# Attention in a four-layer kernel: the split maxima go into the query slot in three SBUF transfers instead of one round trip through DRAM, and the next block's loads are issued behind them

## The chip, the cores and the metric

The kernel is one program on one core of one Trainium2 chip. The metric is the device time of one execution in microseconds (us). Before the change, three runs took 3569.54, 3575.7 and 3576.92 us; the median is 3575.7 us.

## The reference

Four layers run over 32 blocks of 256 tokens with 128 features: a state-space layer and an expert layer, linear attention and experts, softmax attention with low-rank experts, and a scan followed by a small transformer layer with experts. The change touches only the two softmax attentions, `h2` (causal, layer 2) and `h3` (not causal, layer 3). What they compute per block is this (`h3` in the reference's own words; `h2` is the same with a causal mask and low-rank projections):

```python
q, k, v = (heads(q), heads(k), heads(v))        # 16 heads of 8
scores = jnp.einsum('bhqd,bhkd->bhqk', q, k) / jnp.sqrt(jnp.asarray(hd, x.dtype))
attn = jax.nn.softmax(scores, axis=-1)
o = jnp.einsum('bhqk,bhkd->bhqd', attn, v)
return o @ wo.T + bo
```

## The kernel before, in words

`attend(tag, ...)` runs once for `h2` and once for `h3`. The loop is over blocks `b` of 256 tokens (32 of them), software-pipelined over three blocks at once, and written out for each engine by hand: step `b` computes, for each of 16 head positions `h`, the weights of block `b` (`scores`, `weights`, `weigh`), the row maxima of block `b + 2` (`max_scores` on TensorE, `maximum` on VectorE), and the end of block `b - 1` (`turn_sums`, `norm`, `turn_out`, `project_out`, `added`). All engines work through their own list in order; semaphores are all that ties them. A `Signal` named `s["x"]` counts; `at("x", b, k)` is its value after `k` of block `b`'s counts.

Queries and keys are held as three bf16 parts of each number, 48 rows (`KR = 48`) in all, so that a bf16 matmul over 128 partitions gives scores of nearly f32 precision. There are four slots, `sq[u]` and `sk[u]`, each 128 partitions x 16 heads x 256 tokens bf16; block `b` uses slot `b % 4`. Rows 48 to 50 of a query slot (`KR:KM`) are special. Rows 48 to 50 of the key slots hold ones. While a block's maxima are being computed its query rows 48 to 50 are zero. Later they hold the negated maximum of each query, split into three bf16 parts, so that the same matmul gives score minus maximum, ready for `Exp`.

The maxima take this path. VectorE reduces them (`h_nm`); GpSimd splits them into three parts (`split_max`, `h_mpart`); at head position 5 of step `b` TensorE turns the parts of block `b + 1` (`turn_max`, line 2387) and ScalarE copies them to `mT`, 48 partitions (part by head) x 256 tokens (line 2460, signal `mc`). SyncE's queue then stores `mT` to the DRAM tensor `m_parts` (line 2166, signal `mout`), waits for that, and loads `m_parts` into rows 48 to 50 of block `b + 1`'s query slot (line 2168, signal `min`). TensorE's first `scores` of step `b + 1` wait for `min`.

SyncE's queue also loads block `b + 3`: queries (line 2482, 48 x 16 pieces of 512 bytes), keys (line 2483, the same), zeros for rows 48 to 50 (line 2484, copied from a zero part of `sk[0]`) and values with a column of ones (line 2153, 256 pieces of 576 bytes). It does that in step `b` as soon as `weigh` of block `b - 1` is over (signal `pv`), at head position 2. These four transfers count on one signal, `loaded` (64 = 4 x 16). The first `max_scores` of step `b + 1`, at head position 0 right behind the first `scores`, works on block `b + 3` and waits for all 64 (`unit_free`). The steps before block 1 load nothing, since four blocks lie in the slots when the loop starts, and the last three have nothing left to load.

In SyncE's step the loads stand ahead of the two `m_parts` transfers.

Of the kernel before, what the change touches and what calls it, by code (L numbers as in the profile page):

```python
# [33 lines left out]
NH, HD = 16, 8  # L34
# [138 lines left out]
def build(nc, x_in, pack_in, maskb_in, w0_in, w1_in, w3_in, out, ktab, ychan, q_stack, k_stack, ones_rows, v_ones,  # L173
          m_parts, xs1, xs3, ys):
    ctx = ExitStack()
    with ctx:
# [5 lines left out]
        def sig(name, per):  # L182
            return Signal(pool, name, per)

        def sb(name, shape, dt=F32, stack=ctx):
            return stack.enter_context(nc.sbuf_tensor(name, shape, dt))
# [101 lines left out]
        for t, nf, choices in (("e1", F1 // P, 2), ("e3", F3 // P, 1)):  # L288
# [22 lines left out]

        attns = {t: dict(
            {k: sig(f"{t}_{k}", n) for k, n in (
                ("s1", units), ("mx", units), ("mf", 1), ("ms", 3), ("ml", 1), ("mt", 1), ("mc", 1), ("mout", 16), ("min", 16),
                ("vp", 2), ("s2", NH), ("ex", NH), ("pv", 4), ("ev", 2), ("tu", 2), ("rec", 2), ("on", 2), ("ot", 1),
                ("otc", 1), ("out", 1), ("x", 1))},
            loaded=[SlotSignal(pool, f"{t}_loaded{u}", 64, u + 4, 4) for u in range(4)]) for t, units in (("h2", 6), ("h3", 8))}
# [621 lines left out]
        with ExitStack() as st_d:  # L939
# [3 lines left out]
            with ExitStack() as st:  # L943
                mx = sb("d_max", [P, NT], stack=st)
# [950 lines left out]
        with ExitStack() as st1:  # L1895
            h_all = sb("h_all1", [P, NT * P], stack=st1)
            s1, s2 = (sb(f"m1_sel{j}", [P, NT, E1], stack=st1) for j in range(2))
# [31 lines left out]
        KR = 6 * HD  # L1929
        KM = KR + 3  # L1930
# [166 lines left out]
        def attend(tag, causal, dst, w, buffers, load):  # L2097

            s = attns[tag]
# [4 lines left out]
            def at(name, b, k):  # L2104

                return s[name].now(b, k)

            def head(h):

                g, j = h // HG, h % HG  # L2110
                return 8 * (g // 2) + 2 * j + g % 2

            with ExitStack() as st:
                sq, sk, mskb = (buffers[n] for n in ("sq", "sk", "mskb"))
# [5 lines left out]
                mT = sb(f"{tag}_mT", [3 * NH, SEQ], BF16, stack=st)  # L2120
# [13 lines left out]
                def run(eng, step):  # L2134
                    for b in range(-2, 1):
                        step(b, b % SLOTS, b // SLOTS, first=True, turn=b >= -1, body=b >= 0, tail=False)
                    with eng.Fori(0, (NB - 4) // SLOTS) as i:
                        for v in range(1, SLOTS + 1):
                            step(i * SLOTS + v, v % SLOTS, i + v // SLOTS, first=True, turn=True, body=True, tail=True)
                    for b in range(NB - 3, NB + 1):  # L2140
                        step(b, b % SLOTS, b // SLOTS, first=b + 2 < NB, turn=b + 1 < NB, body=b < NB, tail=True)

                def ahead(u, r, n):

                    return (u + n) % SLOTS, r + (u + n) // SLOTS

                with pool.loop_block(NB) as block:
                    k_set = n_chain[0] + 4

                    @block.sync  # L2150
                    def _(sp):
                        def load_values(b, u, up):
                            sp.dma_start(vb[u][:, :, :, :].rearrange("p t h e -> p t (h e)"),
                                         v_ones[ds(b * TPB, TPB)].rearrange("t p w -> p t w")).then_inc(up, 16)

                        def step(b, u, r, first, turn, body, tail):
                            if first and tail and not (isinstance(b, int) and b + 3 >= NB):
                                sp.wait_ge(*at("pv", b, 0))
                                slot = ahead(u, r, 3)[0]
                                load(sp, b + 3, slot, s["loaded"][slot].sem)  # L2160
                                load_values(b + 3, slot, s["loaded"][slot].sem)
                            if turn:

                                sp.wait_ge(*at("mc", b + 1, 1))
                                sp.wait_ge(*at("min", b + 1, 0))
                                sp.dma_start(m_parts.rearrange("a h t -> (a h) t"), mT[:, :]).then_inc(s["mout"].sem, 16)
                                sp.wait_ge(*at("mout", b + 1, 16))
                                sp.dma_start(sq[ahead(u, r, 1)[0]][KR:KM, :, :], m_parts).then_inc(s["min"].sem, 16)

                        for b in range(SLOTS):  # L2170
                            load_values(b, b, first_v[tag])
                        run(sp, step)
# [103 lines left out]
                    def _(pe):  # L2276
# [66 lines left out]
                        def scores(b, u, h):  # L2343

                            if h == 0:
                                pe.wait_ge(*at("min", b, 16))
                            pe.wait_ge(*at("ex", b, h - 1))
                            o, hd = ps_2[:, h % 2, :], head(h)
                            if causal:
                                pe.matmul(o[:, 0:SEQ], sk[u][:, hd, 0:P], sq[u][:, hd, :], start=True, stop=False, skip_group_check=True)  # L2350
                                pe.matmul(o[:, SEQ:SW], sk[u][:, hd, P:2 * P], sq[u][:, hd, P:], start=False, stop=False,
                                          skip_group_check=True)
                                ins = pe.matmul(o.rearrange("p (t q) -> p t q", q=SEQ)[:, :, 0:P], mskb[:, 0:P],  # L2353
                                                mskb[:, 2 * P:3 * P].unsqueeze(1).to_broadcast([P, 2, P]),
                                                start=False, stop=True, skip_group_check=True)
                            else:
                                for t in range(TPB):
                                    ins = pe.matmul(o[:, t * SEQ:(t + 1) * SEQ], sk[u][:, hd, t * P:(t + 1) * P], sq[u][:, hd, :],  # L2358
                                                    start=True, stop=True)
                            ins.then_inc(s["s2"].sem, 1)  # L2360
# [76 lines left out]
                    @block.scalar  # L2437
                    def _(act):
                        def weights(b, h):
                            g, j = h // HG, h % HG  # L2440
                            act.wait_ge(*at("s2", b, h + 1))
                            if j == 0:
                                act.wait_ge(*at("pv", b, g - 1))
                            act.activation(pt[g % 2][:, j, :], ps_2[:, h % 2, 0:SW], ACT.Exp, scale=scale).then_inc(s["ex"].sem, 1)  # L2444

                        def keep_sums(b, k):
                            act.wait_ge(*at("pv", b, 2 * k + 2))
                            act.wait_ge(*at("tu", b, k - 1))
                            act.activation(sums[k][:, :], ps_o, ACT.Copy).then_inc(s["ev"].sem, 1)

                        def step(b, u, r, first, turn, body, tail):
                            for h in range(NH):
                                if body:
                                    weights(b, h)
                                if h == 3 and tail:
                                    keep_sums(b - 1, 1)
                                if h == 5 and turn:
                                    act.wait_ge(*at("mt", b + 1, 1))
                                    act.wait_ge(*at("mout", b + 1, 0))
                                    act.activation(mT[:, :], ps_m[0:3 * NH, :], ACT.Copy).then_inc(s["mc"].sem, 1)  # L2460
                                if h == 11 and body:
                                    keep_sums(b, 0)
                                if h == 12 and tail:
                                    act.wait_ge(*at("ot", b - 1, 1))
                                    act.wait_ge(*at("out", b - 1, 0))
                                    act.activation(oT[:, :], ps_m, ACT.Copy).then_inc(s["otc"].sem, 1)

                        run(act, step)


        stats(x_res)
        heads_in = dict(
            sq=[sb(f"h_sq{u}", [P, NH, SEQ], BF16) for u in range(SLOTS)],
# [47 lines left out]
        with ExitStack() as st2:  # L2521
# [4 lines left out]
            with ExitStack() as st:  # L2526
                s1, s2, ex = (sb(f"m2_sel{j}", [P, NT, E2], stack=st) for j in range(3))
# [445 lines left out]
```

## Time and profile before

| | |
|---|---|
| median of 3 runs | 3575.7 us |
| the profiled execution | 3574.73 us, its span 3572.9 us |
| TensorE (PE) busy | 2609.7 us (73%) |
| VectorE (DVE) busy | 2245.5 us (63%) |
| ScalarE (ACT) busy | 1580.3 us (44%) |
| GpSimd (POOL) busy | 634.1 us (18%) |
| one load of a block | 384 KB queries, 384 KB keys, 24 KB zeros, 144 KB values |
| one store or load of `m_parts` | 24 KB |
| attention `h2`, its loop | about 1880 to 2345 us |
| attention `h3`, its loop | about 2713 to 3185 us |

The profiled execution is within 1 us of the median, so its durations can be used as they are. Times in the rows are from the span's start. A timeline row gives start, duration, engine, line, instruction, output and input, and in brackets the idle time ahead of it with what ended it. SPq is the queue of SyncE: its rows show when a transfer is issued, not when it lands. PE is the matmul, PEld the weight load. Matmuls overlap, so a PE that is busy all the time is not a PE at its peak. In a row of a table by stretches the columns are the stretch, its length, the busy time of PE, PEld, DVE, ACT and POOL with the number of instructions, the TensorE clock that was granted (1.00 is full), the busy share of the DMA engines, and GB/s.

### The profile page before, as it was taken

How to read it: one execution, taken by the hardware profiler on the slowest of the kernel's cores; microseconds unless marked ns; L12 is line 12 of the kernel's file. 1: busy time of each engine (PE TensorE's matmuls, PEld its weight loads, DVE VectorE, ACT ScalarE, POOL GpSimd, SP SyncE). 2: the span in 40 equal slices, each digit the busy share in tenths (PEclk: the TensorE clock that was granted, in tenths of full speed). 3: DMA queues.
4: the chain of work that ended last, by engine and by line, in shares of the span. 5: the costliest groups of instructions: out<-in, count | busy, mean ns of one | idle time of the engine just before them, and what ended most of it. 6: DMA issues, size and time to landing. Idle time of an engine off the chain costs nothing. (4 is left out here: it accounts for less than half of the span.)

```text
span 3572.9 us, 72294 instructions
## 1 busy us (share of the span) xinstructions
PE 2609.7 (73%) x20194; PEld 1892.7 (53%) x20194; DVE 2245.5 (63%) x4945; ACT 1580.3 (44%) x3615; POOL 634.1 (18%) x873
## 2 busy tenths in 40 slices
PE   3546749999987576998339999966565999973280
PEld 1333444459877433998226777756333555552270
DVE  5924966248777422776846666645885777765267
ACT  2503613334364233775235666632253667751253
POOL 0000100000000265554301111100120111102553
PEclk7878959999998687999679999968797999985585
DMA  3096100100091011222494565400097555510123
GB/s 94 7 258 176 53 0 18 35 18 0 0 156 54 20 46 43 70 69 89 152 276 62 71 73 71 57 1 1 0 293 109 69 68 75 71 43 19 53 77 100
DMA packets 335935, 263.34 MB, mean 74 GB/s; under 512 B 23132, under 2 KB 317452, under 8 KB 335308
## 3 DMA queue, kind: packets, MB, share of 16 engines
q1 hardware_dynamic: 314200, 227.03, 31.5%
q0 software_dynamic: 12928, 26.70, 2.2%
q10 hardware_dynamic: 8704, 8.39, 0.8%
q8 instruction: 46, 0.75, 0.1%
q14 instruction: 57, 0.47, 0.0%
HBM read 145.60 MB, written 114.86 MB: 73 GB/s over the span
## 5 line engine op out<-in xcount | busy, mean ns | idle before, releaser
L2444 ACT ACTIVATE h_pt<-h_ps 128x384 f32<-128x384 f32 (+1 forms) x1024 | 543.6, 545 | 306.2 <-PE h_ps L2353 151.8
L2197 DVE TENSOR_REDUCE h_nm<-h_ps 128x4 f32<-128x1024 f32 (+1 forms) x448 | 539.7, 1220 | 163.4 <-PE h_ps L2324 64.0
L1606 POOL DMA_INDIRECT sorted_rows<-e_row,e_pos x192 | 185.1, 964 | 443.4 <-DVE e_row L1585 239.6
L2372 PE MATMUL h_ps_o<-h_pt,h_vp 128*32 128x256 f32 (+1 forms) x4096 | 246.8, 358 | 1.3 <-ACT h_pt L2444 1.3
L1796 POOL DMA_INDIRECT results<-e_y,e_ykey x208 | 211.0, 1015 | 193.6 <-DVE e_y L1785 176.7
L1843 ACT ACTIVATE e_hid<-e_ps_h,e_wt 128x128 f32<-128x128 f32 x688 | 204.3, 369 | 27.7 <-PE e_ps_h L1817 19.0
L2358 PE MATMUL h_ps<-h_sq,h_sk 128*128 128x256 bf16 x1024 | 193.6, 275 | 23.9 <-DMA h_sq<-m_parts 13.6
L1817 PE MATMUL e_ps_h<-e_hT,e_wt 128*128 128x128 f32 x1376 | 201.9, 288 | 6.3 <-issue 2.6
L1825 PE MATMUL e_ps_o<-e_wt,e_hid 128*128 128x128 f32 x1376 | 198.0, 283 | 11.2 <-ACT e_hid L1843 10.4
L1753 DVE TENSOR_SCALAR e_wt<-w 128x1156 f32 (+1 forms) x208 | 140.0, 673 | 98.5 <-DVE e_y L1785 69.8
L1817 PEld LDWEIGHTS e_ps_h<-e_hT,e_wt 128*128 128x128 f32 x1376 | 179.7, 201 | 14.2 <-issue 10.4
L1825 PEld LDWEIGHTS e_ps_o<-e_wt,e_hid 128*128 128x128 f32 x1376 | 178.2, 199 | 15.9 <-ACT e_hid L1843 13.5
L2295 PE MATMUL h_ps<-h_sk,h_sq 128*128 128x256 bf16 x1024 | 157.1, 277 | 39.7 <-DVE h_identb L2179 34.5
L2243 POOL TENSOR_TENSOR h_mpart<-h_nm,h_zero 128x32 bf16<-128x32 f32 x64 | 15.3, 240 | 892.5 <-DVE h_nm L2197 892.5
L2372 PEld LDWEIGHTS h_ps_o<-h_pt,h_vp 128*32 128x32 f32 x4096 | 106.8, 109 | 92.5 <-issue 36.7
L1810 PE MATMUL e_ps_t<-pack,e_xt 128*128 128x128 f32 x208 | 59.2, 286 | 124.9 <-DMA e_xt<-sorted_rows 124.3
L2350 PE MATMUL h_ps<-h_sq,h_sk 128*128 128x256 bf16 x512 | 140.6, 275 | 6.6 <-ACT h_pt L2444 2.8
L2353 PE MATMUL h_ps<-h_mskb 128*128 128x256 bf16 x512 | 139.6, 273 | 0.0
L1140 DVE TENSOR_TENSOR x_hid<-x_gelu,x_ps_u 128x512 f32<-128x512 f32 x64 | 43.4, 688 | 141.8 <-ACT x_gelu L1125 141.8
L2307 PE MATMUL h_ps<-h_sk,h_sq 128*128 128x256 bf16 x512 | 98.2, 274 | 45.7 <-DVE h_identb L2179 44.3
L2358 PEld LDWEIGHTS h_ps<-h_sq,h_sk 128*128 128x128 bf16 x1024 | 81.5, 98 | 93.1 <-ACT h_pt L2444 80.6
L2295 PEld LDWEIGHTS h_ps<-h_sk,h_sq 128*128 128x128 bf16 x1024 | 98.4, 99 | 58.7 <-DVE h_identb L2179 34.7
(435 smaller groups left out, 6170.8 us busy)
## 6 DMA issues: line engine op xcount, KB each, us to landing
h_sq<-q_stack SPq DMA_DIRECT2D x64, 384.0 KB
h_sk<-k_stack SPq DMA_DIRECT2D x64, 384.0 KB
sorted_rows<-pad SPq DMA_DIRECT2D x26, 520.0 KB, 11.7
e_xt<-sorted_rows SPq DMA_DIRECT2D x104, 130.0 KB, 2.2
e_got<-results SPq DMA_DIRECT2D x24, 512.0 KB, 5.9
q_stack<-p_parts SPq DMA_DIRECT2D x32, 384.0 KB, 3.1
k_stack<-p_parts SPq DMA_DIRECT2D x32, 384.0 KB, 3.8
v_ones<-p_v SPq DMA_DIRECT2D x32, 288.0 KB, 2.7
```

The source lines that it names most:

```text
L1606: gp.indirect_dma_start(xs[:, :], bass.IndirectOffsetOnAxis(ap=pos[:, n % choices, tile:tile + 1], axis=0), row[n % ROWS][:, :], None).the ...
L1753: dve.tensor_scalar(wt[j % 4][:, :], w[:, :, :].rearrange("p e w -> p (e w)")[:, ds(at, wc)], 1.0, None, ALU.mult).then_inc(e_w.sem, 1)
L1796: gp.indirect_dma_start(ys[:, :], bass.IndirectOffsetOnAxis(ap=key[m // 4][:, m % 4:m % 4 + 1], axis=0), y[m][:, :], None).then_inc(return ...
L1817: pe.matmul(ps_h[:, k, 0:P], wt[j % 4][:, f * P:(f + 1) * P], hT[j % 4][:, :], start=True, stop=True).then_inc(e_h.sem, 1)
L1825: ins = pe.matmul(o, hid_t[m][:, f, :], wt[m][:, f_dim + f * D:f_dim + (f + 1) * D], start=(f == 0), stop=(f == nf - 1))
L1843: act.activation(hid_t[j % 4][:, f, :], ps_h[:, (j * nf + f) % 4, 0:P], func, bias=wt[j % 4][:, o_b1 + f:o_b1 + f + 1]).then_inc(e_a.sem, 1)
L2197: dve.tensor_reduce(to, got, AX, ALU.max, negate=True).then_inc(s["mx"].sem, 1)
L2295: ins = pe.matmul(ps_1[:, h % 4, q * SEQ:(q + 1) * SEQ], sq[u][:, h, q * P:(q + 1) * P], sk[u][:, h, :], start=True, stop=True)
L2350: pe.matmul(o[:, 0:SEQ], sk[u][:, hd, 0:P], sq[u][:, hd, :], start=True, stop=False, skip_group_check=True)
L2358: ins = pe.matmul(o[:, t * SEQ:(t + 1) * SEQ], sk[u][:, hd, t * P:(t + 1) * P], sq[u][:, hd, :], start=True, stop=True)
L2372: ins = pe.matmul(ps_o[32 * j:32 * (j + 1), q0:], vp[u % 2][:, t, head(HG * g + j), :], pt[g % 2][:, j, t * SEQ:(t + 1) * SEQ - q0], start ...
L2444: act.activation(pt[g % 2][:, j, :], ps_2[:, h % 2, 0:SW], ACT.Exp, scale=scale).then_inc(s["ex"].sem, 1)
```

## The change

Lines 2157 to 2161 of the new kernel take the place of lines 2162 to 2168 of the old one. The detour through `m_parts` and its signal `mout` are gone. `mT` goes straight into the query slot in three transfers, one for each of the three rows: 16 partitions of 512 bytes become one partition of 8 KB. All three count on `min`, which goes to 48. They are issued ahead of the loads of block `b + 3`, so that these loads, the zeroing of rows 48 to 50 and the values come behind them in SyncE's list, and behind its wait for `mc`.

```diff
-                ("s1", units), ("mx", units), ("mf", 1), ("ms", 3), ("ml", 1), ("mt", 1), ("mc", 1), ("mout", 16), ("min", 16),
+                ("s1", units), ("mx", units), ("mf", 1), ("ms", 3), ("ml", 1), ("mt", 1), ("mc", 1), ("min", 48),
@@ SyncE
                         def step(b, u, r, first, turn, body, tail):
+                            if turn:
+
+                                sp.wait_ge(*at("mc", b + 1, 1))
+                                for a in range(3):
+                                    sp.dma_start(sq[ahead(u, r, 1)[0]][KR + a:KR + a + 1, :, :], mT[a * NH:(a + 1) * NH, :]
+                                                 ).then_inc(s["min"].sem, 16)
                             if first and tail and not (isinstance(b, int) and b + 3 >= NB):
                                 sp.wait_ge(*at("pv", b, 0))
                                 slot = ahead(u, r, 3)[0]
                                 load(sp, b + 3, slot, s["loaded"][slot].sem)
                                 load_values(b + 3, slot, s["loaded"][slot].sem)
-                            if turn:
-
-                                sp.wait_ge(*at("mc", b + 1, 1))
-                                sp.wait_ge(*at("min", b + 1, 0))
-                                sp.dma_start(m_parts.rearrange("a h t -> (a h) t"), mT[:, :]).then_inc(s["mout"].sem, 16)
-                                sp.wait_ge(*at("mout", b + 1, 16))
-                                sp.dma_start(sq[ahead(u, r, 1)[0]][KR:KM, :, :], m_parts).then_inc(s["min"].sem, 16)
@@ TensorE, scores
-                                pe.wait_ge(*at("min", b, 16))
+                                pe.wait_ge(*at("min", b, 48))
@@ ScalarE, the copy to mT
-                                    act.wait_ge(*at("mout", b + 1, 0))
+                                    act.wait_ge(*at("min", b + 1, 0))
```

No instruction of TensorE, VectorE, ScalarE or GpSimd moves. On SyncE's queue one step of the loop of `attend` reads so before (ISA and REGISTER_ALU rows are waits and address arithmetic; signal5 is `pv`, signal3 is `mc`, signal2 is `min`, signal4 is `mout`):

```order
L2482 ISA [waits signal5]
L2482 DMA h_sq<-q_stack 48x16x256
L2483 DMA h_sk<-k_stack 48x16x256
L2484 DMA h_sq<-h_sk 3x4096
L2153 ISA
L2153 DMA h_vb<-v_ones 128x2x144
L2164 REGISTER_ALU
L2165 ISA [waits signal2]
L2166 DMA m_parts<-h_mT 48x256 [waits signal3]
L2167 REGISTER_ALU
L2168 DMA h_sq<-m_parts 3x4096 [waits signal4]
```

The same step of SyncE's queue after the change, where the lines of the loads have moved up by one, signal2 is `mc` and signal4 is `pv`:

```order
L2159 REGISTER_ALU
L2161 DMA h_sq<-h_mT 1x16x256 [waits signal2]
L2161 DMA h_sq<-h_mT 1x16x256 x2
L2164 ISA
L2481 ISA [waits signal4]
L2481 DMA h_sq<-q_stack 48x16x256
L2482 DMA h_sk<-k_stack 48x16x256
L2483 DMA h_sq<-h_sk 3x4096
L2153 ISA
L2153 DMA h_vb<-v_ones 128x2x144
```

The four loads have moved from ahead of the wait for `mc` to behind it and behind three transfers; the wait for `mout`, which stood between the last two rows, is gone.

## Rows read from the trace of the kernel before

**Rows 1.** The page, its head.

```profile
span 3572.9 us, 72294 instructions
```

**Rows 2.** Windows of `h2`'s middle, `h3`'s middle and `h3`'s end.

```profile
1922.00:2316.00 394.00, 389.92 (x4668) 288.43 (x4666) 250.29 (x362) 247.24 (x557) 50.21 (x168) 1.00 0.56 70
...
2750.00:3130.00 380.00, 361.72 (x3736) 225.49 (x3734) 298.54 (x401) 264.87 (x533) 47.83 (x160) 1.00 0.56 71
3130.00:3185.00 55.00, 48.13 (x496) 26.91 (x488) 26.36 (x47) 37.59 (x77) 4.40 (x14) 1.00 0.16 21
```

**Rows 3.** Tile `h_sq`, what its matmuls waited for: us, times.

```profile
  DMA h_sq<-m_parts: 17.9, 32
```

**Rows 4.** Timeline of SyncE's queue, one step of `h2` and the next.

```profile
2009.68 0.34 SPq L2482 DMA_DIRECT2D h_sq<-q_stack  x1
...
2011.57 0.41 SPq L2153 DMA_DIRECT2D h_vb<-v_ones  x1
2012.45 0.34 SPq L2166 DMA_DIRECT2D m_parts<-h_mT  x1
2018.86 0.26 SPq L2168 DMA_DIRECT2D h_sq<-m_parts  x1
...
2026.52 0.34 SPq L2166 DMA_DIRECT2D m_parts<-h_mT  x1
```

**Rows 5.** Timeline of ScalarE and TensorE in the same steps of `h2`.

```profile
2011.96 0.36 ACT L2460 ACTIVATE h_mT<-h_ps_m 48x256 bf16<-48x256 f32 x1
...
2021.38 0.38 PE L2307 MATMUL h_ps<-h_sk,h_sq 128*128 128x256 bf16 x2
```

**Rows 6.** Timeline of SyncE's queue and TensorE, one step of `h3`.

```profile
2941.24 0.25 SPq L2168 DMA_DIRECT2D h_sq<-m_parts  x1
...
2943.61 0.39 PE L2358 MATMUL h_ps<-h_sq,h_sk 128*128 128x256 bf16 x2 [0.42 <-DMA h_sq<-m_parts]
...
2943.84 0.60 PE L2295 MATMUL h_ps<-h_sk,h_sq 128*128 128x256 bf16 x4
...
2946.38 0.34 SPq L2482 DMA_DIRECT2D h_sq<-q_stack  x1
...
2949.09 0.34 SPq L2166 DMA_DIRECT2D m_parts<-h_mT  x1
```

**Rows 7.** The same queue and TensorE where the maxima came latest in `h3`.

```profile
2760.04 0.34 SPq L2482 DMA_DIRECT2D h_sq<-q_stack  x1
...
2770.64 0.25 SPq L2168 DMA_DIRECT2D h_sq<-m_parts  x1
...
2772.89 0.39 PE L2358 MATMUL h_ps<-h_sq,h_sk 128*128 128x256 bf16 x2 [1.91 <-DMA h_sq<-m_parts]
...
2775.66 0.34 SPq L2482 DMA_DIRECT2D h_sq<-q_stack  x1
```

**Rows 8.** Tile `h_vb`, issue to landing; then windows of a half microsecond in `h2`.

```profile
DMA to landing us min/median/max: 5.9/7.2/8.3
...
2017.50:2018.00 0.50, 0.50 (x8) 0.41 (x7) 0.00 (x0) 0.33 (x2) 0.00 (x0) 1.00 0.76 107
2018.00:2018.50 0.50, 0.50 (x6) 0.43 (x5) 0.27 (x1) 0.50 (x2) 0.00 (x0) 1.00 0.09 22
```

**Rows 9.** Issues by line (ns min/median/max), and four in a row before `h2`.

```profile
L2484 SPq DMA_DIRECT2D h_sq<-h_sk x64: 708/723/3305, 1853.9 to 3131.5; - x64
L2166 SPq DMA_DIRECT2D m_parts<-h_mT x64: 302/339/345, 1890.7 to 3160.5; - x64
...
1851.07 1.68 SPq L2081 DMA_DIRECT2D h_sk<-ones_rows  x4
```

**Rows 10.** Loads of the loops: count; the last of `h2`, the first of `h3`.

```profile
L2482 SPq MOVE h_sq<-q_stack x56: 29/29/37, 1909.2 to 3130.5; - x56
...
2292.60 0.34 SPq L2482 DMA_DIRECT2D h_sq<-q_stack  x1
...
2745.83 0.35 SPq L2482 DMA_DIRECT2D h_sq<-q_stack  x1
```

## The prediction, made before the result was known

> **What bounds the kernel now.** I first read the head of the page for the span, 3572.9 us [rows 1]; the execution took 3574.7 us, so 1.8 us lie around the span, and it stands 1 us under the median of the runs, 3575.7 us. The change touches only the loops of the two attentions, so next come the windows over their middles [rows 2]: TensorE is busy 389.9 of 394 us in `h2` and 361.7 of 380 us in `h3`, at a granted clock of 1.00. VectorE and ScalarE have a quarter or more free. TensorE sets the pace of both loops, and anything that makes it stop is paid. Third, the view of the tile `h_sq` says what TensorE and its weight loads stopped for: the transfer of the maxima out of `m_parts`, 17.9 us in 32 waits over both attentions [rows 3]. That is the wait which the change aims at, and all there is of it.
>
> Fourth, SyncE's queue beside TensorE, step by step. I call q the moment at which the first load of a step is issued. In a step of `h2` [rows 4] q is 2009.68. The values are issued at q + 1.89, and the store of the maxima at q + 2.77. That store follows ScalarE's copy, which ends at 2011.96 + 0.36 = 2012.32 [rows 5], by 0.13 us, so it is the maxima that are late there and not the queue. The store has landed at 2018.86, q + 9.18, when the second transfer is issued. TensorE starts the maxima of the newly loaded block at 2021.38, q + 11.70 [rows 5].
>
> The loads themselves are the thing to place. The values take 7.2 us in the median from issue to landing [rows 8], and 1.89 + 7.2 makes q + 9.1. The DMA engines bear it out: their share falls from 0.76 to 0.09 at 2018.0, q + 8.3, and the last pieces have still to be acknowledged [rows 8]. So a load needs 9.1 us from its first issue, with the DMA engines full of it, and before the change it is ready 11.7 - 9.1 = 2.6 us ahead of its reader. That margin is what the change draws on.
>
> **The change part by part.**
>
> *The three transfers in place of the round trip.* Before, the maxima arrive so: store, landing 6.4 us later because it stands behind a whole load (2012.45 to 2018.86, rows 4), second transfer, and TensorE goes on 2.25 to 2.4 us after that one's issue (2770.64 to 2772.89 in rows 7, 2941.24 to 2943.61 in rows 6). After, they are issued on an empty queue at the same 0.13 us behind the copy, and even at three times 2.4 us one after another they would be there in 7.2 us, where the next step's first maxima, right behind its first scores, are 2021.38 - 2012.45 = 8.9 us away. The 17.9 us of waiting go. Part of that is the weight load's count beside the matmul's for one and the same stop, so I credit 16 us at most, and that only if nothing else is late at the same place. ScalarE's new wait, for `min` instead of `mout`, is for transfers of the step before and is long met: 0. The wait for 48 instead of 16 costs nothing in itself.
>
> *The loads behind them.* Their issue was q; it becomes q + 2.77 in `h2` (2949.09 - 2946.38 = 2.71 in `h3`, rows 6) plus X, the time in which SyncE issues three transfers. X is not in the trace. An issue of the nearest shapes takes 0.34 us (the store of `mT`) or 0.72 us (the other SBUF to SBUF transfer), and four in a row from DRAM take 1.68 us, 0.42 each [rows 9]. With the gaps and the address arithmetic, X lies between 1.1 us (three at 0.34 and little else) and 2.5 us (three at 0.72 and 0.3). I take 1.5: three at 0.42, the row with transfers back to back, and some 0.25 us between. Then the load lands at q + 2.77 + 1.5 + 9.1 = q + 13.4, and TensorE asks for it at q + 11.7. Behind that wait on TensorE stands all the rest of its step: the scores of head 1, for which ScalarE waits, and the maxima, for which VectorE waits. The cover of 2.6 us is gone and 1.7 us are missing.
>
> *Does it repeat?* Yes, since a circle closes: copy of the maxima at head 5, three issues, the load, the wait at head 0 of the next step, TensorE's work from head 0 to head 5, the next copy. Its length is X + 9.1 + R. R is read from the start of the maxima at head 0 to the next store of `mT`: 2026.52 - 2021.38 = 5.14 us in `h2` [rows 4, 5] and 2949.09 - 2943.84 = 5.25 us in `h3` [rows 6]. So the step is 1.5 + 9.1 + 5.14 = 15.74 us in `h2` and 15.85 us in `h3`. Before, 27 steps of `h2` take from 1909.2 to 2292.60, 14.2 us each, and 27 of `h3` from 2745.83 to 3130.5, 14.25 us each [rows 10].
>
> *Does TensorE catch up?* The trace has a step in which the maxima came late by themselves, and TensorE stood for 1.91 us [rows 7]. That load was issued at 2760.04 and the next at 2775.66, 15.62 us apart: 1.4 us over the mean, and from TensorE's restart at 2772.89 to the next q it took 2.77 us, as in a common step, from 2943.61 to 2946.38 [rows 6]. A stop at this place is handed on in full. The new stop lies a little later, behind the first scores, so that ScalarE works off head 0 meanwhile. That may give back what TensorE spends waiting for it between head 0 and 5: I take 0.05 us in `h2`, where TensorE has almost no gap, and 0.2 us in `h3`, with 0 and 0.5 as the ends.
>
> *The sum.* `h2` loses 15.69 - 14.20 = 1.49 us in a step and `h3` 15.65 - 14.25 = 1.40 us. There are 56 loads inside the loops, 28 in each [rows 10], so 28 x 1.49 + 28 x 1.40 = 42 + 39 = 81 us. The gain on the maxima lies inside that, because the period before contains those waits and the period after doesn't. At the start of the loops, outside these 56 steps, 1 us of waiting for the maxima is saved (of the 16, all but those in the middles). The granted clock stays: in `h3`'s end TensorE is busy 48.1 of 55 us and has 1.00 all the same [rows 2], and 1.5 us in 15.7 is no larger hole than that. Sum: 3574.7 + 81 - 1 = 3654.7 us; against the median of the runs, 1 us more. I say 3655.
>
> The ends: X = 1.1, a load of 8.3 us (the fall of the DMA share) and 0.5 us caught up give a step of 1.1 + 8.3 + 5.2 - 0.5 = 14.1, which is no loss. X = 2.5, a load of 9.3 and nothing caught up give 17.0, or 56 x 2.8 = 157 us more, 3732 us.
>
> **The rivals.**
>
> *The load lands in time, and the gain on the maxima is what is left.* The load would have to be faster without the maxima's store behind it. For: the store and the second transfer leave the DMA queue, and a part of 9.1 us is acknowledgement. Against: the shift of 2.77 us alone is already above the margin of 2.6 us, before any of the three issues, and the departing store is 24 KB beside 936 KB. The time would be 3574.7 - 16 = 3558.7, say 3559 us. It decides where a load takes less than 11.7 - 2.8 - 1.5 = 7.4 us.
>
> *A load at the fabric's rate.* If the DMA engines moved this load at their full rate, it would land some 4 to 5 us after its issue, at q + 9, ahead of its reader, and the time would be the 3559 us of the case above. The rows speak against it: 9.1 us, with the engines busy to the end [rows 8]. [...]
>
> *The issues of the three transfers are dear.* One partition takes all 16 pieces, and if SyncE needs 0.72 us for each, as for the other SBUF to SBUF transfer [rows 9], with its gaps X is 2.5 us and the step 16.7 us, the sum 3574.7 + 28 x 2.45 + 28 x 2.4 = 3711 us. For it: the kind of the transfer. Against it: the 0.72 us stand right behind two large issues, and the store of the same `mT` takes 0.34.
>
> *Nearly nothing.* The load closes up to about 8.3 us and the issues are short, so that the stop costs what the maxima cost before: a step of 14.1 to 14.3 us, 3570 to 3580 us.
>
> **How the numbers follow.** The stop on the loads has 0.88: 0.70 around 3655 (3615 to 3690), 0.18 with dear issues or a longer load, up to 3732. The load in time has 0.06 together with the full rate, of which that has 0.01. Nearly nothing has 0.06. A difference under 0.2%, 7 us, is what a measurement of this kernel can't tell from none. So faster 0.06, the same 0.05, slower 0.89. The range of 8 in 10 is 3603 to 3708: it leaves out the cases without a stop and the far part of the dear ones.
>
> **What would show it.** In the profile after, TensorE's first maxima of a step (line 2306 or 2294) carry an idle time of 1 to 2 us ended by a load of `h_sq`, `h_sk` or `h_vb`, 56 times; the waits for the maxima's transfer are gone; the loads are issued 15.6 to 15.8 us apart and about 1.5 us behind the first of the three transfers; TensorE is at about 90% in both middles at an unchanged clock; nothing outside the two loops moves. I would be wrong if the steps are 14 us apart, if the load lands in clearly less than 9 us from its issue, or if TensorE makes up the stop before head 5.

## The result, and the profile after

The changed kernel takes 3736.6 us in the median of 4 runs (3724.52 to 3739.57), the kernel before 3572.8 us in runs beside it. The ratio is 1.0452, with a 95% interval of 1.0424 to 1.0479. The forecast was 3655 us and a range up to 3708: the direction was right, the loss is twice the forecast one, 164 us instead of 80.

The head of the page of the changed kernel, which answers to [rows 1]:

```profile
span 3733.4 us, 72223 instructions
```

Its windows over the middles of the two loops, with the columns of [rows 2]:

```profile
1922.00:2316.00 394.00, 343.83 (x3876) 248.74 (x3874) 210.73 (x303) 205.09 (x462) 42.22 (x142) 0.95 0.47 58
2850.00:3230.00 380.00, 324.57 (x3078) 199.91 (x3079) 246.21 (x327) 218.06 (x439) 39.18 (x131) 0.91 0.45 57
```

TensorE went from 389.9 to 343.8 busy us in the same 394 us of `h2`. And the granted clock has changed: it is 0.95 and 0.91, where both middles had 1.00.

Who waited for the values' tile `h_vb` in the changed kernel (us, times), and the time to landing, which answers to [rows 8]:

```profile
  PE h_ps L2294: 71.0, 28
  PE h_ps L2306: 58.2, 28
...
DMA to landing us min/median/max: 6.0/7.3/8.4
```

All 56 stops are where they were forecast, on the first maxima of a step. The waits for the maxima's transfer are gone. The time to landing needs care, here and in [rows 8]: only 8 of the 64 transfers of values have one in these traces, the ones that fill the slots ahead of the two loops, because the transfers inside the loops share a semaphore with the other loads. For a load of the loop the next rows give the time. But the stops are 2.08 us in `h2` and 2.54 us in `h3` in the mean, not 1.7.

SyncE's queue in the changed kernel, one step of `h2` to the next, the counterpart of [rows 4]:

```profile
1999.97 1.80 SPq L2161 DMA_DIRECT2D h_sq<-h_mT  x3
2002.06 0.33 SPq L2481 DMA_DIRECT2D h_sq<-q_stack  x1
...
2003.98 0.39 SPq L2153 DMA_DIRECT2D h_vb<-v_ones  x1
2017.53 1.80 SPq L2161 DMA_DIRECT2D h_sq<-h_mT  x3
2019.62 0.33 SPq L2481 DMA_DIRECT2D h_sq<-q_stack  x1
```

The loads start 2002.06 - 1999.97 = 2.09 us behind the first of the three transfers: that is X, forecast as 1.5. Each of the three takes SyncE 0.6 us.

Windows of three single steps of the changed kernel, from one load's issue to the next:

```profile
2002.06:2019.62 17.56, 15.63 (x171) 11.15 (x169) 9.07 (x14) 8.88 (x21) 1.79 (x6) 0.90 0.45 56
1986.04:2002.06 16.02, 14.08 (x171) 10.43 (x169) 9.08 (x14) 8.88 (x21) 1.79 (x6) 1.00 0.49 61
2911.36:2930.40 19.04, 16.24 (x142) 9.74 (x140) 11.33 (x16) 10.08 (x21) 1.79 (x6) 0.82 0.43 52
```

The first two hold the same 171 matmuls. One takes 16.02 us at full clock, its neighbour 17.56 us at 0.90. The third, in `h3`, has 0.82 and 19.04 us. The window into the slow one, by the microsecond:

```profile
2008.00:2009.00 1.00, 1.00 (x11) 0.70 (x8) 0.66 (x2) 0.49 (x1) 0.00 (x0) 1.00 1.19 115
2009.00:2010.00 1.00, 0.00 (x0) 0.00 (x0) 1.00 (x2) 0.49 (x1) 0.00 (x0) 1.00 0.85 101
2010.00:2011.00 1.00, 0.07 (x1) 0.08 (x2) 0.38 (x2) 0.00 (x0) 0.70 (x3) 1.00 0.05 8
2011.00:2012.00 1.00, 1.00 (x10) 0.88 (x11) 0.00 (x0) 0.26 (x1) 0.26 (x2) 0.95 0.00 0
2012.00:2013.00 1.00, 1.00 (x12) 0.43 (x13) 0.85 (x1) 0.63 (x2) 0.00 (x0) 0.50 0.00 0
2013.00:2014.00 1.00, 1.00 (x17) 0.39 (x10) 0.38 (x1) 0.09 (x1) 0.00 (x0) 0.50 0.00 0
2014.00:2015.00 1.00, 1.00 (x6) 0.81 (x7) 0.26 (x1) 0.00 (x0) 0.79 (x2) 0.50 0.00 0
2015.00:2016.00 1.00, 1.00 (x12) 0.86 (x11) 0.29 (x2) 0.76 (x2) 0.04 (x1) 0.84 0.00 0
```

TensorE stands for 1.93 us and starts again at 2010.93, 8.87 us after the load's first issue. Some 0.97 us later the clock goes from 1.00 to 0.50, the 1.2 GHz level, for some 3.4 us, while TensorE is busy all the time. The same sixteen weighing matmuls in the timeline of TensorE, the stop between them:

```profile
2006.62 0.86 PE L2371 MATMUL h_ps_o<-h_pt,h_vp 128*32 128x256 f32 x16
...
2010.93 0.39 PE L2306 MATMUL h_ps<-h_sk,h_sq 128*128 128x256 bf16 x2 [1.93 <-DMA h_vb<-v_ones]
...
2012.49 1.51 PE L2371 MATMUL h_ps_o<-h_pt,h_vp 128*32 128x256 f32 x16
```

They take 0.86 us ahead of the stop and 1.51 us behind it. So a stop here is paid by its length and, in many steps, a second time by the clock. I divided all 27 steps between two loads in each loop by their clock. In `h2`, 14 steps at 1.00 take 16.14 us in the mean and 13 at 0.90 or 0.91 take 17.7; in `h3`, 6 at 1.00 take 16.0, 19 at 0.90 take 17.5 and 2 at 0.82 take 19.0. Against the old 14.20 and 14.25 us [rows 10], the circle at full clock costs 28 x 1.94 + 28 x 1.79 = 104 us, and the clock 28 x (16.90 - 16.14) + 28 x (17.27 - 16.04) = 56 us (16.90 and 17.27 are the means of all steps). The sum is 160 of the 160.5 us between the two profiled spans.

### The profile page after: what moved, and what is told of

The parts are those of the page before. It is cut to its first block and busy times, and to the rows that moved or that the text cites. A ratio compares the mean times of both kernels' runs of the same rounds, so it can differ in the third digit from the quotient of the medians.

```text
span 3733.4 us, 72223 instructions
## 1 busy us (share of the span) xinstructions
PE 2662.5 (71%) x20194; PEld 1919.5 (51%) x20194; DVE 2251.2 (60%) x4945; ACT 1579.3 (42%) x3615; POOL 632.4 (17%) x873
## 5 line engine op out<-in xcount | busy, mean ns | idle before, releaser
L2371 PE MATMUL h_ps_o<-h_pt,h_vp 128*32 128x256 f32 (+1 forms) x4096 | 272.4, 388 | 1.3 <-ACT h_pt L2443 1.3
L2294 PE MATMUL h_ps<-h_sk,h_sq 128*128 128x256 bf16 x1024 | 166.7, 289 | 109.1 <-DMA h_vb<-v_ones 71.0
L2357 PE MATMUL h_ps<-h_sq,h_sk 128*128 128x256 bf16 x1024 | 199.4, 288 | 6.0 <-ACT h_pt L2443 4.4
L2306 PE MATMUL h_ps<-h_sk,h_sq 128*128 128x256 bf16 x512 | 101.4, 281 | 103.1 <-DMA h_vb<-v_ones 58.2
L2349 PE MATMUL h_ps<-h_sq,h_sk 128*128 128x256 bf16 x512 | 143.5, 280 | 2.1 <-ACT h_pt L2443 1.7
L2357 PEld LDWEIGHTS h_ps<-h_sq,h_sk 128*128 128x128 bf16 x1024 | 90.8, 102 | 65.0 <-ACT h_pt L2443 51.1
```

Source lines behind the costliest of these rows:

```text
L2294: ins = pe.matmul(ps_1[:, h % 4, q * SEQ:(q + 1) * SEQ], sq[u][:, h, q * P:(q + 1) * P], sk[u][:, h, :], start=True, stop=True)
L2371: ins = pe.matmul(ps_o[32 * j:32 * (j + 1), q0:], vp[u % 2][:, t, head(HG * g + j), :], pt[g % 2][:, j, t * SEQ:(t + 1) * SEQ - q0], start ...
```

## The experiments

Theory 1: the loss is the later start of the loads, which closes a circle; its size is the issue time of three transfers (0.6 us each), and behind a long stop comes a lower clock. The rivals: the new SBUF to SBUF transfers cost by themselves; or the clock falls for another reason than the stop. All ratios are to the kernel before, run on the same chip beside each experiment. It took 3524.6, 3574.2 and 3524.4 us in the three groups of runs, and what makes these 50 us is not known, so only ratios are compared.

**The hole filled.** In TensorE's step, ahead of the maxima:

```diff
+                                if first and tail and body and h == 0:
+                                    pe.wait_ge(*at("ex", b, 0))
+                                    for _ in range(18):
+                                        pe.matmul(ps_2[:, 1, 0:P], identb[:, :], identb[:, :], start=True, stop=True)
```

> The changed kernel, with 18 small bf16 matmuls (identity times identity, 128 columns, into a score bank that the next scores overwrite) issued by TensorE at head 0 of each step that waits for a load, ahead of that wait. They take about 0.11 us each, 2.0 us in all, and so fill the stop of about 2 us and should not lengthen it. Theory 1 (the stop is paid twice: once by its length, and again in those steps in which the granted clock falls to 0.50 for about 3.4 us behind it): the clock is 1.00 in nearly all steps, the steps are 16.0 to 16.2 us, and the time is 3573 + 56 x 1.85 = about 3676 us. Theory 2 (the clock falls for another reason, or the slow steps come from the new transfers): nothing changes, about 3737 us.

Measured: ratio 1.0330 (1.0312 to 1.0347), against 1.0452. From its timeline of TensorE, and the windows of both middles:

```profile
2002.73 1.18 PE L2434 MATMUL h_ps<-h_identb 128*128 128x128 bf16 x18
...
2004.90 0.39 PE L2306 MATMUL h_ps<-h_sk,h_sq 128*128 128x256 bf16 x2 [0.99 <-DMA h_vb<-v_ones]
```

```profile
1922.00:2316.00 394.00, 369.04 (x4507) 277.03 (x4508) 219.44 (x316) 214.57 (x484) 44.64 (x150) 1.00 0.48 60
2800.00:3180.00 380.00, 346.14 (x3750) 228.38 (x3754) 266.66 (x356) 236.44 (x477) 42.06 (x140) 1.00 0.49 61
```

The 18 matmuls took 1.18 us and not 2.0, so half of the stop was filled; I had taken the pace of matmuls twice as wide. It was enough: all 54 steps are at clock 1.00, 16.27 us in `h2` and 16.04 in `h3`. The loads and the transfers are unchanged, and useless work made the kernel 1.2% faster. That shows that the clock's fall comes from the stop. Its price is about 43 us by the two ratios, which were measured apart and whose intervals leave some 12 us to either side, and 28 x 0.63 + 28 x 1.23 = 52 us by the steps of the two profiled executions.

**The order alone.** The round trip through `m_parts` stays as before; only the loads move behind it:

```diff
-                            if first and tail and not (isinstance(b, int) and b + 3 >= NB):
-                                ... (wait for pv, the four loads)
                             if turn:
                                 ... (store to m_parts, wait, load of m_parts)
+                            if first and tail and not (isinstance(b, int) and b + 3 >= NB):
+                                ... (wait for pv, the four loads)
```

> The kernel before, with the loads moved behind the two m_parts transfers, and no other change: the round trip through DRAM stays. Theory 1 (what costs is that the loads start later): the loads start 0.34 + 1.1 (landing on an empty queue, 1.44 from issue) + 0.25 + 0.3 = about 2.0 us behind the first transfer of the maxima, as late as in the changed kernel (2.1), so the steps and the clock are as there and the time is 3725 to 3745 us. Rival (the three SBUF to SBUF transfers cost, by contention or by landing slowly): the time stays near the old one, under 3620 us.

Measured: ratio 1.0472 (1.0455 to 1.0490), the loss of the changed kernel with none of its transfers. In its queue the loads start 2.0 us behind the store:

```profile
2000.98 0.34 SPq L2161 DMA_DIRECT2D m_parts<-h_mT  x1
2002.41 0.26 SPq L2163 DMA_DIRECT2D h_sq<-m_parts  x1
2002.97 0.34 SPq L2482 DMA_DIRECT2D h_sq<-q_stack  x1
```

Here too 11 of 27 steps of `h2` and 19 of 27 of `h3` are below full clock. On an empty queue the dreaded round trip takes 1.43 us to the second issue. So the loss needs none of the new transfers: their kind counts only by the time in which SyncE issues them.

**One row, two rows.** `for a in range(1)` and `range(2)` in place of 3, with `min` at 16 and 32: the other rows of the query slot keep their zeros.

> The changed kernel with only the first of the three transfers, so that rows 49 and 50 of the query slot keep their zeros and the maxima have one bf16 part: it leaves out two thirds of the maxima's transport. The loads start 0.6 + 0.3 = 0.9 us behind the first transfer instead of 2.1. Theory 1: the circle is 1.2 us shorter, steps of 14.9 us at full clock, a stop of 0.7 to 0.8 us; and the clock does not fall behind so short a stop: 3573 + 56 x 0.7 = about 3612 us. If a short stop makes the clock fall as often as a long one, about 3612 + 37 x 1.6 = 3671 us. Rival (the loads' order and not the issue time costs): near 3737 us.

> The changed kernel with two of the three transfers (row 50 keeps its zeros, the lowest bf16 part of the maxima is left out). Their issue takes about 1.2 us and the loads start 1.5 us behind the first one: just the value that the prediction took for three. Theory 1 (the prediction failed in two terms, the issue time and the clock): steps of 15.4 to 15.5 us at full clock, 56 x 1.25 = 70 us, or 2.0% over the kernel before, and a clock that falls in few steps (0 to 12 of 56, up to 18 us more, 2.5%). If the clock term goes with the stop's length in a straight line, about 15 to 18 of the 56 steps fall and it is 2.7%.

Measured: one row 1.0112 (1.0095 to 1.0129), forecast 3612 of 3573, 1.011; steps of 14.96 us in `h2` and 14.83 us in `h3`, all at clock 1.00. Two rows 1.0252 (1.0236 to 1.0268), between the two cases named. At full clock its steps are 15.55 and 15.34 us, which makes 28 x 1.35 + 28 x 1.09 = 68 us; 1 step of 27 in `h2` and 11 of 27 in `h3` fell below. This is the X that the prediction took for three transfers. Each row costs about 0.6 us in every step, on top of it the clock.

**One transfer for all three rows.** `min` is at 16 here too.

```diff
-                                for a in range(3):
-                                    sp.dma_start(sq[ahead(u, r, 1)[0]][KR + a:KR + a + 1, :, :], mT[a * NH:(a + 1) * NH, :]
-                                                 ).then_inc(s["min"].sem, 16)
+                                sp.dma_start(sq[ahead(u, r, 1)[0]][KR:KM, :, :].rearrange("a h t -> a (h t)"), mT[:, :]).then_inc(s["min"].sem, 16)
```

> The changed kernel with one transfer for all three rows, 48 partitions of 512 bytes into 3 partitions of 8 KB, and the loads behind it. If its issue takes 0.6 us like one of the three, the loads start 0.9 us behind the first transfer: the same as with one row, about 3612 us by theory 1 with an unchanged clock. If it needs an issue as dear as three (1.8 us), 3737 us.

Measured: 1.0169 (1.0152 to 1.0187), over the 1.011 expected. Its queue:

```profile
2003.09 0.77 SPq L2160 DMA_DIRECT2D h_sq<-h_mT  x1
2004.18 0.33 SPq L2479 DMA_DIRECT2D h_sq<-q_stack  x1
```

The one issue takes 0.77 us and not 0.6, the loads start 1.09 us behind it, and the steps are 15.34 us in `h2` and 15.15 in `h3`; 2 of 54 are below full clock. One issue is much cheaper than three, yet the order still loses.

**The values apart, and the zeros first.** The values get a signal of their own, for which GpSimd waits; TensorE waits for 48. In a second kernel the zeros of rows 48 to 50 are issued ahead of the queries as well.

```diff
-                                load_values(b + 3, slot, s["loaded"][slot].sem)
+                                load_values(b + 3, slot, s["vals"][slot].sem)
-                                gp.wait_ge(*s["loaded"][u].last(r, 64))
+                                gp.wait_ge(*s["vals"][u].last(r, 16))
-                                pe.wait_ge(*s["loaded"][u].last(r, 64))
+                                pe.wait_ge(*s["loaded"][u].last(r, 48))
```

> The changed kernel with a semaphore of its own for the values, so that TensorE's maxima wait for queries, keys and zeros alone (48) and GpSimd for the values (16). The values are issued last, 1.9 us behind the queries, and are 144 of 936 KB. Theory 1 (each microsecond by which the awaited load lands earlier shortens the circle by one): the stop is 0.5 to 1.3 us shorter, the steps 14.9 to 15.6 us at full clock, the clock falls seldom, and the time is 1.5 to 2.6% over the kernel before instead of 4.5%. Rival (zeros or keys land last, the values don't matter): no change, 4.5%.

> As the run with a semaphore of its own for the values, and with the zeros of a load issued ahead of its queries and keys instead of behind them. There the zeros ended TensorE's wait. If what TensorE waits for is the zeros transfer itself, three rows of 8 KB that are slow in landing, the wait ends 0.5 to 1 us earlier and the time falls from 3.8% over the kernel before to 2.2 to 3.0%. If it is the queries and keys (768 of 936 KB, with the DMA engines full) and the zeros were merely last in the queue, the wait is then ended by the keys, the queries start 0.7 us later behind the zeros' issue, and the time stays at 3.8% or goes up to 4.5%.

Measured: 1.0384 (1.0370 to 1.0399) for the first, where I had expected 1.5 to 2.6% over the kernel before: the steps at full clock are only 0.25 us shorter in `h2` and 0.13 in `h3`. TensorE's matmuls on `h_sq` now waited for this, in us and times:

```profile
  DMA h_sq<-h_sk: 124.6, 58
```

Since the values have a signal of their own here, the trace has the landings of most of them, 50 of 64:

```profile
DMA to landing us min/median/max: 5.6/7.0/8.6
```

With the zeros first the ratio is 1.0484 (1.0467 to 1.0502), and they waited for this:

```profile
  DMA h_sk<-k_stack: 160.7, 58
```

So it is the bulk of queries and keys that lands late, the small transfers were only last, and another 0.7 us ahead of the bulk is lost like any other. I had expected up to 4.5% here.

**The loads first, the direct transfers behind.** SyncE's order of before, the transfers of after (and once with the single transfer):

```diff
                             if first and tail and not (isinstance(b, int) and b + 3 >= NB):
                                 ... (wait for pv, the four loads)
+                            if turn:
+
+                                sp.wait_ge(*at("mc", b + 1, 1))
+                                for a in range(3):
+                                    ... (the three transfers from mT)
```

> The changed kernel with SyncE's order put back: the loads of block b + 3 first, at the moment of the kernel before, and then the three direct transfers of the maxima. Theory 1 (the loss is all in the start of the loads, the direct transfers are a small gain): no stop on a load, clock 1.00 in all steps of both middles, the wait for the maxima gone or nearly so (they land with the load, at q + 9.3 to 9.7, ahead of the first scores at q + 11.3): 0.2 to 0.45% under the kernel before (16 us of waiting at most). Rival (the direct transfers themselves cost, or are of no use since they queue behind the load): the same as before or slower.

> As the run with the order put back, but with one direct transfer of all three rows instead of three, behind the loads. Its issue takes 0.76 us instead of 1.8, and neither stands in anyone's way any more, so theory 1 expects the same time as with three, within 0.1%: 0.2 to 0.45% under the kernel before.

Measured: with three transfers 0.9914 (0.9900 to 0.9927), with one 0.9908 (0.9894 to 0.9921). Both beat the kernel before and the changed one, and by twice what I expected. The queue with one transfer, and the windows over the middles:

```profile
2002.12 0.33 SPq L2479 DMA_DIRECT2D h_sq<-q_stack  x1
...
2004.77 0.76 SPq L2165 DMA_DIRECT2D h_sq<-h_mT  x1
2016.01 0.33 SPq L2479 DMA_DIRECT2D h_sq<-q_stack  x1
```

```profile
1922.00:2316.00 394.00, 393.15 (x4757) 294.28 (x4746) 248.73 (x364) 251.98 (x571) 49.20 (x168) 1.00 0.54 67
2740.00:3095.00 355.00, 351.11 (x3674) 225.86 (x3666) 291.63 (x393) 259.69 (x524) 46.05 (x156) 1.00 0.58 72
```

The steps are 13.90 us in `h2` and 13.54 us in `h3`, all at full clock, and TensorE is busy for 99% of both middles. No stop on `h_sq` by a transfer is left in either kernel. The gain in the steps is 28 x 0.30 + 28 x 0.71 = 28 us, where the view had shown 17.9 us of stops [rows 3]; by the ratio it is 33 us, with an interval of 28 to 38.

How often the clock fell, by the mean recorded stop on a load (us) and the steps below full clock, of 27:

| kernel | `h2` stop, steps | `h3` stop, steps | ratio |
|---|---|---|---|
| loads first, one transfer | none, 0 | none, 0 | 0.9908 |
| one row | 0.88, 0 | 1.43, 0 | 1.0112 |
| single transfer | 1.29, 0 | 1.75, 2 | 1.0169 |
| two rows | 1.53, 1 | 2.00, 11 | 1.0252 |
| changed kernel, stop half filled | 1.02, 0 | 1.40, 0 | 1.0330 |
| values apart | 1.89, 6 | 2.39, 21 | 1.0384 |
| changed kernel | 2.08, 13 | 2.54, 21 | 1.0452 |
| order alone | 2.34, 11 | 2.76, 19 | 1.0472 |
| values apart, zeros first | 2.53, 12 | 3.01, 21 | 1.0484 |

The length of a stop doesn't decide alone. In the changed kernel's `h2` the stops of the 13 steps with a fall are 1.93 to 2.54 us long and those of the 14 others 1.89 to 2.23 us; in `h3` they are 2.29 to 3.45 us and 2.10 to 2.72 us.

## Why the prediction was right in sign and wrong in size

**The circle: right.** "The loads behind them" and "Does it repeat?" held in every part: 56 stops on the first maxima, none elsewhere, loads that need about 9 us (2002.06 to TensorE's restart at 2010.93 is 8.87), and a step of X + 8.9 + R. With the measured X that is 2.09 + 8.87 + 5.05 = 16.0 us (R from 1994.92, TensorE's restart in the step before, to 1999.97), and the steps at full clock take 16.14. The order alone reproduces the loss, and the order put back removes it. The 7.2 us from [rows 8] were a lucky hit: they belong to 8 transfers of values ahead of the loops, 5.9 to 8.3 us long. That a load of the loop needs about 9 us rests on the fall of the DMA share at q + 8.3, on these 8.87 us, and on the 7.0 us of the run with the values apart.

**X: mis-sized.** I took three issues at 0.42 us and 0.25 us between, 1.5 us; they take 0.6 us each and 0.29 us to the next issue, 2.09 us. The row I chose by, four transfers back to back, was from DRAM; the dear neighbour in [rows 9], also SBUF to SBUF at 0.72 us, was the nearer kind, and its rival was given 0.18. This term is 56 x 0.59 = 33 us. The run with two rows has the X of the prediction, and its steps at full clock cost 68 us where the prediction had 81: a little was caught up or landed earlier, which of the two isn't shown. So at full clock the changed kernel costs 104 us, not 81.

**The clock: the step that failed.** "The granted clock stays" was argued from one window, the end of `h3`, where TensorE is busy 48.1 of 55 us at 1.00 [rows 2]. A share over 55 us doesn't tell in how many pieces the idle time lies. The one stop of 1.91 us in [rows 7], behind which the clock stayed full, was a second true and misleading witness: in the changed kernel a stop of that size is followed by a full clock in some steps and by 0.50 for 3.4 us in others. The term was put at nothing, and it measured 56 us by the steps; the half-filled stop gave 43 us of it back by the ratio and 52 by the steps. With the 23 us more at full clock (104 for 81) that makes 79 of the 80 us by which the span went beyond the forecast. I can't tell why one of two like steps keeps its clock.

**The gain on the maxima: too small by half.** "I credit 16 us at most" took the recorded stops for the whole price. With the loads where they were, the direct transfers bring 28 us in the steps, and the kernel 0.9%. The round trip goes with longer steps also where TensorE shows no stop on it: the mean step of `h3` lost 0.71 us, its recorded stop 0.5 at most, and the 6 of 27 steps of `h3` before the change that have no such stop of over 0.15 us take 13.96 us in the mean, against 13.54 us now. In `h3`'s middle TensorE's idle time went from 18.3 of 380 us [rows 2] to 3.9 of 355, that is 0.54 us less in a step. Its weight loads waited less for ScalarE's weights. The two rows are the waits in these windows, before and with the single transfer behind the loads (us, times, longest):

```profile
PEld h_ps L2358 <- ACT h_pt L2444: 64.2, 158, 1.2
...
PEld h_ps L2355 <- ACT h_pt L2441: 44.2, 130, 0.4
```

That shows where the rest lies; which engine carried it wasn't tried.

**The rivals.** "The load lands in time" and the load at the fabric's rate fell at once: of the landings in the run with the values apart none came under 5.6 us, and no run shows a whole load in the 4 to 5 us that this rival needs. "The issues are dear" was right in its mechanism: of the rivals its X of 2.5 us and 3711 us came nearest to the result, and it lacked the clock.

## What to carry to other kernels

Where an order within a queue is changed to help a small late transfer, work out the margin of the large one that it is put ahead of; here it was 2.6 us, and 4.9 us were taken. A new stop of an engine that was never idle is to be priced twice where it comes to about 2 us: by its length and by a lower clock behind it, and some useless matmuls in the stop tell the two apart. If the transfer saved is good and the order bad, do one without the other: direct transfers behind the loads gave 0.9%, and the full change lost 4.5%.

## What the runs showed of the hardware

- A stop of TensorE of about 2 us in otherwise full work is followed in a part of the cases (34 of 54 steps of the changed kernel) by a granted clock of 0.50 for 3.4 us; in the step shown it starts 0.97 us after TensorE is at work again, and 1.54 us are lost (17.56 against 16.02). Eighteen matmuls of 1.18 us in all inside the stop prevented it in all 54 steps.
- SyncE needs 0.6 us to issue one SBUF to SBUF transfer of 16 pieces of 512 bytes into one partition, and 0.76 us for one of 48 pieces into three; the store of the same 48 rows to DRAM takes 0.34.
- With no load ahead in the queue, a direct transfer of a row lands in 1.9 us in the median (changed kernel) and the DRAM store in 1.4 (order alone). Behind a load they take 6.2 us (three transfers behind the loads) and 6.4 us (kernel before).
